# A state-space scan with a routed feed-forward layer: the router's steps spread over all slots of a chunk, one product moved to GpSimd, down products four slots behind

## The reference, cut to what matters

```python
xn = layernorm(x)
# scan, per token t, channel d, state n
dt = soft_clamp(softplus(xn @ Wdt.T + bdt), 0.001, 0.1, 0.5)
h = exp(soft_clamp(dt * A)) * h + dt * (xn @ WB.T) * xn        # h: [d, n]
h = h * minimum(20 / norm(h), 1)
y = sum_n(h * (xn @ WC.T)) + Dp * xn
# router
scores = sigmoid(xn @ router_w.T); sfc = scores + bias         # 64 experts in 8 groups
group_scores = top2(sfc in each group).sum(); keep the 4 best groups
masked = where(group kept, sfc, 0); picks = top8(masked)
c = scores[picks] / (scores[picks].sum() + 1e-20) * 2.5
routed = sum_e c[:, e] * (relu(xn @ up[e])**2 @ down[e])
shared = relu(xn @ shared_up)**2 @ shared_down
out = x + y + routed + shared
```

## Time and profile before

| | us |
|---|---|
| median of 3 runs (571.67 to 572.81) | 571.87 |
| the profiled execution | 574.56 |
| its span, first to last instruction | 572.8 |
| TensorE busy | 508.6 (89%) |
| VectorE busy | 496.0 (87%) |
| ScalarE busy | 470.4 (82%) |
| GpSimd busy | 469.3 (82%) |

### The profile page before, as it was taken

The page is one execution under the profiler, slowest core; times in us unless marked ns, Lnnn a source line. Parts: engine busy times, 40 slices in busy tenths (PEclk is TensorE's granted clock), DMA queues, the critical chain, the costliest instruction groups (busy, mean ns, idle before and its releaser), DMA issues.

```text
span 572.8 us, 7918 instructions
## 1 busy us (share of the span) xinstructions
PE 508.6 (89%) x1666; PEld 278.0 (49%) x1666; DVE 496.0 (87%) x1158; ACT 470.4 (82%) x922; POOL 469.3 (82%) x430
## 2 busy tenths in 40 slices
PE   2158899998898988999899998999989998999996
PEld 1034445554454545565455544555445554555552
DVE  3657899899988899899998899888998899979984
ACT  2768798799886998888986998879988889988872
POOL 2389898897888979897988978889897979968762
PEclk9999999999999999999999999999999999999999
DMA  8956865887869877987678877697769877699951
GB/s 200 326 166 229 277 258 197 318 291 259 247 191 348 276 261 232 347 271 262 247 239 307 304 264 248 197 364 264 272 216 321 300 249 246 219 318 353 317 189 37
DMA packets 65649, 149.32 MB, mean 261 GB/s; under 512 B 14048, under 2 KB 31040, under 8 KB 65600
## 3 DMA queue, kind: packets, MB, share of 16 engines
q1 hardware_dynamic: 63728, 147.07, 76.3%
q10 hardware_dynamic: 1872, 1.75, 0.9%
HBM read 143.03 MB, written 5.77 MB: 260 GB/s over the span
## 4 chain that ended last, share of the span: by engine, by line
POOL 28%; issue 22%; DVE 18%; PE 14%; ACT 8%; DMA 8%; SPq 1%; POOLq 1%; DVEq 0%; ACTq 0%
POOL yacc L546 10%; DMA bc_rows<-bc_dram 7%; PE DN L1088 7%; POOL bc_rows L537 6%; DVE DC L944 4%; DVE relu L885 4%; POOL xn L444 3%; DVE g L831 3%; DVE bc_rows L897 3%; PE U L1038 2%; PE U L1039 2%; PE U L1040 2%; ACT act L715 2%; POOL rstd L438 1%; POOL rest L527 1%
## 5 line engine op out<-in xcount | busy, mean ns | idle before, releaser
L1088 PE MATMUL DN<-act,down 128*128 128x512 f32 x512 | 261.9, 593 | 1.9 <-ACT act L715 1.9
L715 ACT ACTIVATE act<-relu 128x512 f32<-128x512 f32 x272 | 169.5, 623 | 44.6 <-DVE relu L885 38.3
L885 DVE SCALAR_TENSOR_TENSOR relu<-U,gate_rows 128x512 f32<-128x512 f32 x256 | 173.6, 678 | 34.0 <-PE U L1040 17.8
L546 POOL TENSOR_TENSOR yacc<-yacc,bc_rows 128x512 f32<-128x512 f32 x120 | 154.5, 1287 | 44.9 <-DVE bc_rows L897 44.9
L1038 PE MATMUL U<-x_hi,up_hi 128*128 128x512 f32 x256 | 163.4, 638 | 23.5 <-DVE relu L885 22.5
L537 POOL TENSOR_TENSOR bc_rows<-dtx_all,bc_rows 128x512 f32<-128x512 f32 x128 | 164.4, 1285 | 20.2 <-DMA bc_rows<-bc_dram 20.2
L944 DVE TENSOR_TENSOR_SCAN DC<-DC,carry,bc_rows 128x512 f32<-128x512 f32 x96 | 122.7, 1278 | 0.0
L1088 PEld LDWEIGHTS DN<-act,down 128*128 128x128 f32 x512 | 95.3, 188 | 28.7 <-ACT act L715 6.6
L1038 PEld LDWEIGHTS U<-x_hi,up_hi 128*128 128x128 f32 x256 | 48.2, 188 | 113.7 <-DVE relu L885 70.1
L1039 PE MATMUL U<-x_lo,up_hi 128*128 128x512 f32 x256 | 101.2, 395 | 0.0
L1040 PE MATMUL U<-x_hi,up_lo 128*128 128x512 f32 x256 | 101.1, 395 | 0.0
(11 more groups left out here) (113 smaller groups left out, 501.5 us busy)
## 6 DMA issues: line engine op xcount, KB each, us to landing
bc_rows<-bc_dram SPq DMA_DIRECT2D x128, 512.0 KB, 6.0
gate_rows<-gate_dram SPq DMA_DIRECT2D x128, 512.0 KB, 4.8
xs<-in_L_attn_x SPq DMA_DIRECT2D x8, 256.0 KB, 5.6
down<-in_L_ffn_down_w SPq DMA_DIRECT2D x8, 256.0 KB, 4.9
xr<-in_L_attn_x SPq DMA_DIRECT2D x8, 256.0 KB, 5.6
rest_kept_dram<-rest SPq DMA_DIRECT2D x8, 256.0 KB, 4.3
out<-res SPq DMA_DIRECT2D x8, 256.0 KB, 4.5
dtx_all<-in_L_ffn_up_w SPq DMA_DIRECT2D x3, 512.0 KB, 5.6
```

What stands on the lines that cost most here:

```text
L546: g.tensor_tensor(yacc[:, :], yacc[:, :], c_rows[:, (c * N + n) % BUFS, :], ALU.add).then_inc(yacc_done, 1)
L715: a.activation(act_at(c, slot), relu[:, slot % 2, :], ACT.Square).then_inc(sq_done, 1)
L885: v.scalar_tensor_tensor(out=relu[:, slot % 2, :], in0=U[slot % 2][:, :], scalar=0.0, in1=gate_rows[:, k // 2 % SBUFS, slot % 2, :], op0=A ...
L1088: mm(DN[:, :], w, act_at(c, slot), start=slot == 0, stop=slot == SLOTS - 1).then_inc(down_done, 1)
```

## The change

The slot numbers of `prep` are new on every engine. Five of its slots, numbered -5 to -1 (statistics, `rstd`, `xn`), are run in the last five slots of the chunk before the one they were in (`due`); in chunk 0, which has to do all of the preparation of chunk 1, they are run at its start and a few numbers are doubled later. The remaining steps are spread from slot 1 to slot 28; `cc`'s transposes and the gates' copy and store are now functions of their own, in slots 29 (PE) and 30 (ACT). The marks `g1c` and `picked` compare with the constant that the match wrote, instead of with a second tensor. The product of picks and scores is on GpSimd, ahead of `cc`, and DVE waits for it before `wsum`. `LAG` is 4, `ABUFS` 5. `yacc` has two halves, by the parity of the chunk. On SP the gate loads stand one row load later, `xs` is loaded in mid chunk, and the stores of rest and result one and three rows earlier. `result` is in slot 12 instead of 20, `out_mm` in 11 instead of 19.

```diff
-    LAG = 3
-    ABUFS = 4
+    LAG = 4
+    ABUFS = 5
-        yacc = sb("yacc", [P, CT])
+        yacc = sb("yacc", [P, 2, CT])
+        FRONT = 5
+        TAKEN = -3.0e38
+        def due(c, slot):
+            if c == 0:
+                if slot < 21:
+                    mine = [slot - 4] if slot else [-FRONT, -4]
+                elif slot < 25:
+                    mine = [2 * slot - 25, 2 * slot - 24]
+                else:
+                    mine = [slot]
+                mine = [(1, p) for p in mine if p < SLOTS - FRONT]
+            else:
+                mine = [(c + 1, slot)] if slot < SLOTS - FRONT else []
+            if slot >= SLOTS - FRONT:
+                mine.append((c + 2, slot - SLOTS))
+            return [(pc, p) for pc, p in mine if pc < NCH]
...
# SP, transfers
-                    if n == 0 and not last:
-                        x_next(c)
+                    if n == 5 and c + 2 < NCH:
+                        x_next(c + 1)
...
                     rows(c, n)
-                    if n:
-                        gates_in(c, n - 1)
+                    if n > 1:
+                        gates_in(c, n - 2)
+                gates_in(c, N - 2)
                 gates_in(c, N - 1)
...
# GpSimd, prep
-                if slot == 22:
+                if slot == 24:
                     pool.wait_ge(picked_ready, pc + 1)
...
+                    g.tensor_tensor(masked[:, :, :], picked[:, :, :], sig[:, :, :], ALU.mult).then_inc(psig_ready, 1)
...
-                if slot == 23:
+                if slot == 26:
                     pool.wait_ge(wsum_ready, pc + 1)
...
-                if slot == 12:
+                if slot == 11:
                     pool.wait_ge(sig_ready, pc + 1)
...
# ScalarE
-                    if not last:
-                        prep(c + 1, slot)
+                    if slot == 30 and not last:
+                        gates_out(c + 1)
+                    for pc, p in due(c, slot):
+                        prep(pc, p)
...
# VectorE, prep
-                if slot in (13, 13.5, 14, 14.5):
-                    k = int(2 * (slot - 13))
+                if slot in (11, 12, 13, 14):
+                    k = slot - 11
...
-                if slot == 15.5:
+                if slot == 14.5:
                     op(v.tensor_tensor, g1a[:, :], g8[:, :, 0], g8[:, :, 1], ALU.add)
...
-                    v.tensor_tensor(g1c[:, :], g1a[:, :], g1b[:, :], ALU.not_equal).then_inc(groups_ready, 1)
+                    v.tensor_scalar(g1c[:, :], g1b[:, :], TAKEN, None, ALU.is_equal).then_inc(groups_ready, 1)
...
-                if slot == 21.5:
+                if slot == 23.5:
                     ch.wait()
-                    v.tensor_tensor(picked[:, :, :], picked[:, :, :], masked[:, :, :],
-                                    ALU.not_equal).then_inc(picked_ready, 1)
-                if slot == 22:
-                    dve.wait_ge(picked_ready, pc + 1)
-                    ch.then(v.tensor_tensor(masked[:, :, :], picked[:, :, :], sig[:, :, :], ALU.mult))
-                if slot == 22.5:
-                    ch.wait()
+                    v.tensor_scalar(picked[:, :, :], picked[:, :, :], TAKEN, None, ALU.is_equal).then_inc(picked_ready, 1)
+                if slot == 25.5:
+                    dve.wait_ge(psig_ready, pc + 1)
                     v.tensor_reduce(wsum[:, :], masked[:, :, :], axis=AX.X, op=ALU.add).then_inc(wsum_ready, 1)
...
-                    if slot == 20 and not first:
+                    if slot == 12 and not first:
                         result(c - 1)
...
# TensorE, chunk
-                    if 3 < slot:
-                        down_mm(c, slot - 3)
-                    elif slot < 3 and not first:
-                        down_mm(c - 1, SLOTS - 3 + slot)
+                    if slot == LAG + 1:
+                        down_mm(c, 0)
+                    if slot > LAG:
+                        down_mm(c, slot - LAG)
+                    elif slot < LAG and not first:
+                        down_mm(c - 1, SLOTS - LAG + slot)
...
-                    if slot == 19 and not first:
+                    if slot == 11 and not first:
                         out_mm(c - 1)
+                    if slot == 29 and not last:
+                        cc_mm(c + 1)
```

## The result

The changed kernel takes 594.57 us (median of 4 runs, 590.13 to 596.62) against 572.34 beside it (4 runs): 1.0375 times as long, 95% interval 1.0341 to 1.0409. The forecast was 566.1 with a range from 555 to 577, so both sign and range were missed. The profiled run has 596.62 us and a span of 594.8.

What follows compares the result with a forecast made beforehand. No single engine bounds it; PE waits 5.7 of 66.7 us a regular chunk, mostly for DVE's relu. Six chunks at -1.2, chunk 0 +1.5, prologue +0.3, (g) -0.4: -5.8, span 567.0, median 566.1 us, range 555 to 577.

Steps and rivals of the forecast that it cites:

- (f): Statistics, rstd and xn moved to the last five slots of the chunk before: -0.4 us a chunk, bounds 0 and -1.0.
- The POOL rival: POOL's load grows, its operations after DVE start late, marks wait: 582 us, 577 with half of it; chance 0.10.
- (a): Product of picks and scores leaves DVE for POOL: -1.3 us a chunk, POOL's 0.73 us taken as free.
- (b): The two marks become one-input comparisons with a constant: +0.3 us a chunk together, bounds -0.1 and +2.5.
- (c): Sum g1a on DVE moves to slot 15, between relu and scan: +0.2 us a chunk, bounds 0 and 1.3.
- (d): First maxima move from slot 13 to 11; DVE's wait for sfc becomes 1.0 us: +0.7 a chunk, bounds 0 and 2.
- (e): Picks on DVE stretched from slots 20-23 to 20-26, flattening the pile: -0.7 us a chunk, between zero and -1.7.
- (g): Down products on PE four slots behind, five buffers: -0.4 us in all, bounds 0 and -6.6.
- (h): Gates' transposes, copy and store come later: taken at nothing, the other end 3.3 us a chunk.
- the gates' rival: Gates' store lands in 6.6 to 8.5 us, so each chunk's first relu products wait: +16, 582 us; chance 0.13.
- Chunk 0: First chunk, with rstd and xn of one more chunk and the product on POOL: +1.5 us, bounds -1 and +4.
- Prologue: Before the first chunk, the product is now in series with the sum of weights: +0.3 us.

Runs made afterwards that it cites:

- late-middle kernel: Changed kernel with the steps from xn's transposes (now slot 3) to the group match, and the result's transposes, put back about where the kernel before has them: 559.23 us.
- the filler: Changed kernel with twelve matmuls, result thrown away, added on PE in each chunk ahead of its wait for xn: 582.86 us, ratio 1.0186.
- LAG 3: Changed kernel with down products three slots behind U and four act buffers, as before: 591.01 us, ratio 1.0328.
- slot 1: The late-middle kernel with only PE's transposes of xn moved from slot 3 to 1: 587.71 us, ratio 1.0284.

## Why the prediction was wrong, point by point

**The step that failed is (f).** It said that xn would be ready "hardly before" the transposes ask, from 10.5 us of POOL work in 9.4, and then booked -0.4 with bounds of 0 and -1.0. That sum started POOL's row at slot 28. The trace shows POOL without a gap since slot 18, so at slot 28 it was already behind, and xn came 3.2 us late for slot 1. A bound on the loss side was missing altogether, and what a late xn costs wasn't asked: U(2) behind the transposes, the clock behind the wait. With the rest of the late-middle kernel, the early front with the transposes in slot 1 is 14.5 us slower than the old front with the transposes in slot 3 (587.71 less 573.25), +2.4 us in each of six chunks where -0.4 was booked; with the transposes in slot 3, where xn is ready, the early front gives -2.3 (14.0 over six). The slots of the transposes and of xn against each other make the sign; moving either of them turned it.

**The clock** was dismissed because it was 1.00 before. That says nothing of a kernel in which PE has a new wait of 3 us. Its share of the loss, some 12 us by the filler, is in no term and no rival.

**The POOL rival** (577 to 583) had the right engine and the wrong place: POOL operations late after DVE and slow marks. Late marks were found in chunk 0 only; the backlog reached PE through xn. Its 10% and its price were too small.

The other steps, each in its turn:

- (a) -1.3 a chunk: -1.0 measured in the late-middle kernel, with the product at 730 ns on POOL against the 727 assumed. In the kernel as changed it has the other sign, +13.9 us in all: "I take that as free" hung on the same slack of POOL as (f).
- (b) +0.3 a chunk: the marks' means went from 418 to 468 ns and from 300 to 379. These are the groups after, and three instances of the first, in the prologue, chunk 0 and chunk 3:

```profile
L899 DVE TENSOR_SCALAR picked<-picked 128x256 f32<-128x256 f32 x8 | 3.7, 468 | 0.1
...
L883 DVE TENSOR_SCALAR g1c<-g1b 128x32 f32<-128x32 f32 x8 | 3.0, 379 | 0.1
```

```profile
29.04 0.29 DVE L899 TENSOR_SCALAR picked<-picked 128x256 f32<-128x256 f32 x1
...
90.78 1.08 DVE L899 TENSOR_SCALAR picked<-picked 128x256 f32<-128x256 f32 x1
...
299.88 0.38 DVE L899 TENSOR_SCALAR picked<-picked 128x256 f32<-128x256 f32 x1
```

  The means hide two cases. In the regular chunks the marks take 0.37 to 0.49 us and 0.17, against 0.42 and 0.18 before, so they cost nothing there; in chunk 0 they take 1.08 and 0.90, the former beside a y sum on POOL that ran from 90.44 to 91.71, and +1.4 us falls on that chunk. By the Trainium skill, VectorE: DVE Perf Modes, section "The perf-mode tier table", the one-input comparison on fp32 would run at twice the rate. The shortest instance agrees: 0.29 us in the prologue against 0.43 for the two-input one at the same place before, close to the 0.14 less that the prediction worked out.
- (c) +0.2: g1a's mean went from 213 to 346 ns, +0.13. (d) The wait for sfc was to become 1.0: it is 1.12 to 1.18 in the regular chunks. Its price of +0.7 a chunk was too high: the closer middle as a whole costs 6.9 us (594.6 less 587.7), and 4.6 where nobody waits long for xn (569.2 less 564.7), of which by the stretches 1.0 is in the prologue, 1.3 in chunk 0 and 0.3 in each regular chunk. What sfc's wait is of it was not tried alone.
- (e) -0.7 a chunk: 4.3 us in all, -0.6 a chunk, the mark's meeting with POOL in it. (g) -0.4 in all: 0 to +3.6. (h) taken at nothing: SP's order, the one part that was tried alone, is nothing; the store's landing went from 2.3/6.6/8.5 to 2.2 with nothing issued just ahead of it, and the gates' rival falls.
- Chunk 0: +1.5 forecast, +0.4 measured. Prologue: +0.3 forecast, +1.7 measured; PE's wait for cc there is 17.2 us against 15.6 before, and 16.3 with the late middle, with the product on either engine. So the product is not what lengthens it; the 0.7 that the late middle leaves was not looked into.

With xn's end in front of one more product and y sum the changed kernel takes 569.2 us, 3.1 above the forecast; its span of 567.3 and its regular chunks of 65.3 us are within 0.3 of the forecast's 567.0 and 65.5. The rest of the sum was right as a sum, partly by luck: (b), (d) and chunk 0 were priced too high and the prologue too low, (g) gave nothing, and the parts don't add up one by one. One order on one queue made it useless.

## What to carry to other kernels

When a step moves to an engine's busy stretch, don't count that engine's load from the new slot on: follow its gapless row back to the last real gap, and add the length. Then ask what stands behind the consumer in its own in-order queue, and give a late arrival a price on the loss side. If the consumer is TensorE, price a wait of some 2 us or more twice, once for itself and once, as a chance, for the clock.

## What the runs showed of the hardware

A wait of PE inside busy work made a fall of its granted clock from 1.00 to 0.50 (1.2 GHz) likely, and not certain. The kernel before has waits of 1.63 and 2.43 us for xn without a fall. In the profiled executions of the five kernels in which xn comes 3.2 us late (changed, LAG 3, slot 1, and the two with the front one slot earlier) the clock fell at 22 of 25 such waits, and at three of five waits of 2.6 us. With the product on VectorE and with the old front in slots 0 to 2 it fell at two of six waits of 1.87 to 1.95 us and at none of five of 1.49 to 1.56; at waits under 0.7 us it never fell. A fall behind one of these waits lasted some 4 or some 7 us. Matmuls whose result is thrown away, put into the wait, kept the clock up and paid 11.7 us in 595.

A comparison with a constant, 128x256 in fp32 on VectorE, took 0.29 to 0.49 us at seven of eight places of the changed kernel and 1.08 at the eighth, where a sum on GpSimd ran beside it and ended 0.15 us earlier; with the picks in their old slots, beside a product on GpSimd, it took 0.79 us (median).
